# Reordering the head of a transformer layer: loads, statistics, weight splits and the first projection

## The chip, the cores and the metric

One core of a Trainium2 chip runs the whole kernel. The metric is the device time of one launch in microseconds, as the median of several runs. Lower is better.

## The reference

The input `x` holds 4 sequences (the code calls them blocks) of 256 tokens with 256 features. What is computed:

```
xn  = (x - mean) / sqrt(var + 1e-5)              # per token
q,k,v = xn @ Wqkv.T                              # 16 heads of 16 features
s   = softmax(q k^T / 4) v @ Wproj.T + bproj     # attention per sequence and head
h   = gelu(xn @ proj1.T + b1)                    # 1024 hidden features
g   = silu(h @ proj2.T + b2)
out = x + s * g
```

Everything is float32. The kernel gets that accuracy from TensorE in three products: each operand is split into a high part (rounded to the fast 32-bit matmul type) and a low part (the rest), and hi·hi, lo·hi and hi·lo are summed in PSUM.

## The kernel before, in words

Each engine has a program of its own, and a list that `build_order` writes out by hand gives all of them the same order of steps. Steps that matter here: `XT b` (transpose the normalised block `b` on TensorE), `QK h i` (project queries, i = 0 and 1, or keys, i = 2 and 3, of half `h`, which is 512 tokens or two blocks), `V`, `F1` and `F2` (values and the two layers of the feed-forward net), `S` (scores of two heads for the row maximum), `ST` (scores again, transposed, for the exponentials), `PV` and `PJ` (attention output and its projection).

The head of the kernel, which is what is changed, goes like this.

- SyncE (SP) issues the loads in the order x0, x1, the three thirds of `Wqkv` (queries, keys, values; 256 KB each, as an x block is), x2, x3, then `w1` (1 MB), and two small DMAs that write the rows of ones. ScalarE (ACT) issues three loads of the biases on its own queue at the very start; two of them are broadcast to 128 partitions.
- VectorE (DVE) does `norm_stats(b)` (two bn_stats, two bn_aggr, one add) and `norm_apply(b)` (two tensor_scalar, L484) for a block. Between them GpSimd (POOL) computes the reciprocal root in `rsqrt(b)` (L331).
- ACT makes the high part of a weight third in `split_wqkv(c)` (L379), POOL its low part (`wql`, L339).
- After `XT b` on TensorE (L632), ACT writes the high part `xTh` (L389) and DVE the low part `xTl` (L506).
- `QK 0 0` fills a PSUM bank of 512 columns in two products of 256 columns. ACT writes its high part to `stage` (L396), DVE its low part (L514), and only after both does SP issue three DMAs (L296) that restack the 128 rows of `stage` into groups of 16 partitions of `qs` or `ks`. There are 24 such DMAs of 256 KB, twelve for each half; `S` of a half waits for all its twelve (semaphore `stacked`, 192).
- SP works its list strictly in order: the twelve stack DMAs of half 0, the loads of `w2` and `wp`, then the twelve of half 1.

The order of DVE in the head before is: stats 0, stats 1, apply 0, apply 1, `xTl` of block 0, `xTl` of block 1, stats 2, stats 3, low part of `QK 0 0`, apply 2, low part of `QK 0 1`, apply 3. The order of POOL is: root 0, root 1, `wql` of the three thirds, root 2, root 3, `w1l`. The order of ACT is: high part of thirds 0 and 1, `xTh` of block 0, high part of third 2, `xTh` of block 1, then the high parts of `QK`.

Of the kernel before, what the change touches and what calls it, by code (L numbers as in the profile page):

```python
# [5 lines left out]
B, SQ, E = 4, 256, 256  # L6
NH, HN = 16, 16
F = 1024
P = 128
TOK = B * SQ  # L10
TT = TOK // P
HALF = TOK // 2
KC = E // P
# [79 lines left out]
def layer_kernel(nc, x, wqkv, w1, b1, w2, b2, wp, bp, out):  # L93
# [8 lines left out]
    with ctx:  # L102
# [168 lines left out]
        @block.sync  # L271
        def _(sp):

            x_t = x.rearrange("(b p t) e -> p b (t e)", p=P, t=2)
            out_t = out.rearrange("(b p t) e -> p b t e", p=P, t=2)
            for b in range(2):
                sp.dma_start(xs[:, 2 * b:2 * b + 2, :], x_t[:, b, :]).then_inc(x_in[b], 16)  # L277
            for c in range(3):
                sp.dma_start(wqkv_raw[:, c], wqkv[c]).then_inc(wqkv_in[c], 16)
            for b in range(2, B):  # L280
                sp.dma_start(xs[:, 2 * b:2 * b + 2, :], x_t[:, b, :]).then_inc(x_in[b], 16)
            sp.dma_start(w1_raw[:], w1).then_inc(w1_in, 16)
            sp.wait_ge(ones_ready, 1)
            for par in range(2):
                sp.dma_start(ks[64 * par + STK:64 * par + STM, :, :].bitcast(f32)
                             .rearrange("p h (b t) -> p (h b) t", t=SQ),
                             ones[0:2, None, :].to_broadcast([2, HP * B, SQ])).then_inc(ones_rows, 16)
            for h in range(2):
                cols = slice(h * HALF, (h + 1) * HALF)
                for i in range(4):  # L290
                    stack, parts = (qs, (0, 0, 1)) if i < 2 else (ks, (0, 1, 0))
                    sp.wait_ge(qk_hi, 4 * h + i + 1)
                    sp.wait_ge(qk_lo, 4 * h + i + 1)
                    for n, part in enumerate(parts):
                        row = 64 * (i % 2) + HN * n
                        sp.dma_start(stack[row:row + HN, :, cols].bitcast(f32),  # L296
                                     stage[:, h, i, part, :].bitcast(f32)).then_inc(stacked[h], 16)
                if h == 0:
                    sp.dma_start(w2_raw[:], w2).then_inc(w2_in, 16)
                    sp.dma_start(wps[:], wp).then_inc(wp_in, 16)  # L300
            for b in range(B):
                sp.wait_ge(m_hi, b + 1)
                sp.wait_ge(m_lo, b + 1)
                for qt in range(2):
                    for part in range(2):
                        c = b * SQ + qt * P
                        sp.dma_start(qs[STK + part:P:64, :, c:c + P].bitcast(f32),
                                     mm[qt * NH:(qt + 1) * NH, b % 2, part, :].bitcast(f32)).then_inc(m_rows[b], 16)
            sp.wait_ge(f1_made, 2 * FC)
            sp.dma_start(xb[:].rearrange("p (b t) e -> p b (t e)", t=2), x_t).then_inc(x_again, 16)  # L310
            for u in range(TT):
                sp.wait_ge(fin_done, u + 1)
                sp.dma_start(out_t[:, u // 2, u % 2, :],
                             fin[:, u % 4, :]).then_inc(stored[u], 16)
            for u in range(TT):
                sp.wait_ge(stored[u], 16)
# [3 lines left out]
        def _(pool):  # L320
# [8 lines left out]
            def rsqrt(b):  # L329
                pool.wait_ge(veps_done, b + 1)  # L330
                nc.gpsimd.tensor_tensor(rstd[:, 2 * b:2 * b + 2], veps[:, 2 * b:2 * b + 2],  # L331
                                        mhalf[:, 2 * b:2 * b + 2], ALU.pow).then_inc(rstd_done, 1)

            pool.wait_ge(mhalf_set, 1)
            rsqrt(0)
            rsqrt(1)
            for c in range(3):
                pool.wait_ge(wqkv_hi, c + 1)
                nc.gpsimd.tensor_tensor(wql[:, c], wqkv_raw[:, c], wqh[:, c].bitcast(f32),  # L339
                                        ALU.subtract).then_inc(wqkv_lo, 1)  # L340
            rsqrt(2)
            rsqrt(3)
            for kc in range(KC):
                pool.wait_ge(w1_hi, kc + 1)
                nc.gpsimd.tensor_tensor(w1l[:, kc, :], w1_raw[:, kc, :], w1h[:, kc, :].bitcast(f32),
# [22 lines left out]

        @block.scalar
        def _(act):  # L370
            act.dma_start(b1s[:], b1).then_inc(bias_in, 16)
            act.dma_start(b2s[:], b2.to_broadcast([P, E])).then_inc(bias_in, 16)
            act.dma_start(bps[:], bp.to_broadcast([P, E])).then_inc(bias_in, 16)
            act.wait_ge(warm_set, 1)
            nc.scalar.activation(rc[0:1, 0, 0, 0:1], warm[0:1, 0:1], ACT.Gelu)

# [2 lines left out]
                nc.scalar.activation(wqh[:, c], wqkv_raw[:, c], ACT.Copy).then_inc(wqkv_hi, 1)  # L379

            split_wqkv(0)
            split_wqkv(1)
            n_qk = n_v = n_f1 = n_mt = n_bt = 0
            for s in order:
                if s[0] == "XT":
                    b = s[1]
                    act.wait_ge(xt_made, b + 1)
                    for kc in range(KC):
                        nc.scalar.activation(xTh[:, kc, b * SQ:(b + 1) * SQ], xt_bank(b, kc),  # L389
                                             ACT.Copy).then_inc(xt_hi, 1)  # L390
                    if b == 0:
                        split_wqkv(2)
                elif s[0] == "QK":
                    h, i = s[1:]
                    act.wait_ge(qk_made, n_qk + 1)
# [71 lines left out]
        def _(dve):  # L467
# [25 lines left out]

            nc.vector.memset(warm[:], 0.0).then_inc(warm_set, 1)
            norm_stats(0)
            norm_stats(1)
            norm_apply(0)
            norm_apply(1)
            n_qk = n_mt = 0
            for s in order:  # L500
                if s[0] == "XT":
                    b = s[1]
                    cols = slice(b * SQ, (b + 1) * SQ)
                    for kc in range(KC):
                        dve.wait_ge(xt_hi, KC * b + kc + 1)
                        nc.vector.tensor_tensor(xTl[:, kc, cols], xt_bank(b, kc),  # L506
                                                xTh[:, kc, cols].bitcast(f32), ALU.subtract).then_inc(xt_lo, 1)
                    if b == 1:
                        norm_stats(2)
                        norm_stats(3)  # L510
# [77 lines left out]
        def _(pe):  # L588
# [18 lines left out]
            def wait_bank(s):  # L607
# [5 lines left out]
                else:  # L613
                    wait_free(pe, t_uses, t_free, s, 1)

            def warm_up():

                for _ in range(WARM):
                    nc.tensor.matmul(T[:, 0:HALF // 2], warm[:, 0:P], warm[:], start=True, stop=True)
# [4 lines left out]
            for s in order:  # L624
                if s[0] == "XT":
                    b = s[1]
                    if b >= 2:
                        pe.wait_ge(xt_lo, KC * (b - 1))
                    for t in range(2):
# [4 lines left out]
                    last.then_inc(xt_made, 1)  # L634
                elif s[0] == "QK":
                    h, i = s[1:]
                    pe.wait_ge(wqkv_hi, i // 2 + 1)
                    wait_free(pe, g_uses, g_free, s, 3)

                    cuts = [(0, SQ), (1, SQ)] if (h, i) == (0, 0) else [(h, HALF)]  # L640
                    for n, width in cuts:
                        cols = slice(n * width, (n + 1) * width)
                        seen = KC * (cols.stop // SQ - 1)
                        last = product(G[:, g_bank[s], n * width % HALF:n * width % HALF + width],
                                       lambda kc, a: (wqh, wql)[a][:, i // 2, kc, (i % 2) * P:(i % 2 + 1) * P],
                                       lambda kc, a: (xTh, xTl)[a][:, kc, cols], range(KC),
                                       rhs_hi=(xt_hi, seen), lhs_lo=(wqkv_lo, i // 2 + 1), rhs_lo=(xt_lo, seen))
                    last.then_inc(qk_made, 1)
                elif s[0] == "V":
                    h, p = s[1:]  # L650
                    pe.wait_ge(wqkv_lo, 3)
# [146 lines left out]
```

## Time and profile before

| | |
|---|---|
| runs of the kernel before | 163.93, 164.27, 165.26 us, median 164.27 |
| profiled execution, first to last instruction | 162.8 us |
| mean granted TensorE clock in it | 0.951 of full |
| TensorE busy / VectorE / ScalarE / GpSimd | 139.1 / 87.5 / 78.8 / 50.8 us |
| DMA | 13.28 MB in 7440 packets |

The span of the profiled execution is the time from its first to its last instruction. The time of a run holds something around it as well: 164.27 - 162.8 = 1.5 us, taken as fixed. Times in the sections below are counted from the start of the span.

### The profile page before, as it was taken

What the parts mean: (1) busy time and instruction counts of PE and PEld (TensorE: products, weight loads), DVE (VectorE), ACT (ScalarE), POOL (GpSimd) and SP (SyncE); (2) the same over time, 40 slices, a digit from 0 to 9 for tenths busy, and PEclk for the clock granted to TensorE, in tenths of its full rate; (3) what the DMA queues carried; (4) which work ended last, traced back from release to release, by engine and by line L of the source; (5) the groups of instructions that cost most, each with busy time, mean ns of one, the idle gap of its engine ahead of it and who ended that gap; (6) DMA issues with size and microseconds to landing.
All of it is one profiled execution on the core that took longest, in us unless ns stands there. A gap on an engine that the chain in (4) does not pass through costs nothing.

```text
span 162.8 us, 2711 instructions
## 1 busy us (share of the span) xinstructions
PE 139.1 (85%) x1028; PEld 100.7 (62%) x1028; DVE 87.5 (54%) x170; ACT 78.8 (48%) x115; POOL 50.8 (31%) x53
## 2 busy tenths in 40 slices
PE   7589799200199999999999999999999999999990
PEld 5378698100186666887876667865766666565570
DVE  2569935100046868787976867225245525645663
ACT  3074844100065566111136667787567756788600
POOL 3374920000039766300006666007942003300000
PEclk9999999975569999999999999999999999999997
DMA  5992999999999999960000000053000100001001
GB/s 130 259 380 48 140 119 121 119 120 122 238 202 122 123 124 123 123 78 1 10 2 2 0 8 4 2 154 114 0 0 8 60 0 4 9 26 38 32 30 67
DMA packets 7440, 13.28 MB, mean 82 GB/s; under 512 B 900, under 2 KB 2564, under 8 KB 7172
## 3 DMA queue, kind: packets, MB, share of 16 engines
q1 hardware_dynamic: 6996, 12.85, 45.8%
q10 hardware_dynamic: 432, 0.27, 1.4%
q8 instruction: 8, 0.13, 0.4%
q14 instruction: 4, 0.03, 0.1%
HBM read 5.51 MB, written 1.05 MB: 40 GB/s over the span
## 4 chain that ended last, share of the span: by engine, by line
PE 58%; DMA 21%; SPq 13%; DVE 3%; ACT 2%; issue 1%
PE G L603 31%; DMA ks<-stage 17%; SPq L296 12%; PE G L728 10%; PE SC L696 9%; DMA wqkv_raw<-wqkv 4%; PE SC L676 4%; PE T L737 2%; DVE xs L484 2%; PE G L744 1%; ACT stage L396 1%; DVE fin L582 1%; SPq L277 0%; ACT hG L428 0%; DVE stage L514 0%
## 5 line engine op out<-in xcount | busy, mean ns | idle before, releaser
L523 DVE TENSOR_REDUCE negm<-SC 128x4 f32<-128x1024 f32 x32 | 38.6, 1224 | 29.8 <-PE SC L676 29.4
L446 ACT ACTIVATE PT<-SC 128x1024 f32<-128x1024 f32 x32 | 32.7, 1023 | 11.1 <-PE SC L696 10.7
L354 POOL TENSOR_TENSOR hTl<-hG,hTh 128x512 fp32r<-128x512 f32 x16 | 20.5, 1284 | 29.0 <-ACT hTh L432 29.0
L676 PE MATMUL SC<-ks,qs 48*128 48x256 f32 x128 | 15.5, 331 | 14.9 <-DMA ks<-stage 14.9
L676 PEld LDWEIGHTS SC<-ks,qs 48*128 48x128 f32 x128 | 9.6, 191 | 22.5 <-DMA ks<-stage 15.3
L728 PE MATMUL G<-PT,VA 128*17 128x256 f32 x256 | 16.9, 382 | 0.3 <-DVE cd L535 0.3
L428 ACT ACTIVATE hG<-G,b1s 128x512 f32<-128x512 f32 x16 | 11.0, 688 | 12.1 <-PE G L603 12.1
L696 PE MATMUL SC<-qs,ks 50*128 50x256 f32 x128 | 16.1, 329 | 0.0
L603 PE MATMUL G<-w2h,hTh 128*128 128x256 f32 x64 | 15.2, 319 | 0.2 <-ACT hG L428 0.2
L696 PEld LDWEIGHTS SC<-qs,ks 50*128 50x128 f32 x128 | 9.5, 184 | 7.3 <-issue 5.0
L535 DVE COPY cd<-G 128x256 f32<-128x256 f32 x16 | 6.8, 425 | 12.4 <-PE G L728 12.1
L350 POOL TENSOR_TENSOR w2l<-w_raw,w2h 128x1024 fp32r<-128x1024 f32 x2 | 4.7, 2384 | 26.1 <-ACT w2h L415 26.1
L603 PE MATMUL G<-w2h,hTl 128*128 128x256 f32 x64 | 12.8, 282 | 0.0
L603 PE MATMUL G<-w2l,hTh 128*128 128x256 f32 x64 | 12.8, 282 | 0.0
L603 PEld LDWEIGHTS G<-w2h,hTh 128*128 128x128 f32 x64 | 9.7, 189 | 3.2 <-POOL hTl L354 0.4
L603 PE MATMUL G<-xTh,w1h 128*128 128x512 f32 x32 | 11.6, 445 | 0.0
L364 POOL TENSOR_TENSOR bg<-gate,bps 128x256 f32<-128x256 f32 x8 | 5.8, 729 | 17.5 <-DVE gate L491 16.6
L432 ACT ACTIVATE hTh<-hG 128x512 fp32r<-128x512 f32 x16 | 10.1, 632 | 0.5
L603 PE MATMUL G<-xTh,w1l 128*128 128x512 f32 x32 | 10.0, 394 | 0.0
L603 PE MATMUL G<-xTl,w1h 128*128 128x512 f32 x32 | 9.9, 392 | 0.0
L603 PEld LDWEIGHTS G<-w2l,hTh 128*128 128x128 f32 x64 | 9.9, 191 | 0.0
L415 ACT ACTIVATE w2h<-w_raw 128x1024 fp32r<-128x1024 f32 x2 | 2.0, 1048 | 16.3 <-DMA w_raw<-w 16.3
(83 smaller groups left out, 225.3 us busy)
## 6 DMA issues: line engine op xcount, KB each, us to landing
qs<-stage SPq DMA_DIRECT2D x12, 256.0 KB, 19.3
ks<-stage SPq DMA_DIRECT2D x12, 256.0 KB, 23.1
w_raw<-w SPq DMA_DIRECT2D x2, 1024.0 KB, 15.5
xs<-x SPq DMA_DIRECT2D x4, 256.0 KB, 6.1
xb<-x SPq DMA_DIRECT2D x1, 1024.0 KB, 5.5
out<-fin SPq DMA_DIRECT2D x8, 128.0 KB, 1.7
wqkv_raw<-wqkv SPq DMA_DIRECT2D x3, 256.0 KB, 7.0
wps<-wp SPq DMA_DIRECT2D x1, 256.0 KB, 24.5
```

Source lines behind the costliest of these rows:

```text
L296: sp.dma_start(stack[row:row + HN, :, cols].bitcast(f32), stage[:, h, i, part, :].bitcast(f32)).then_inc(stacked[h], 16)
L354: nc.gpsimd.tensor_tensor(hTl[:, n % FC, :], hG[:, n % FC, :], hTh[:, n % FC, :].bitcast(f32), ALU.subtract).then_inc(h_lo, 1)
L364: nc.gpsimd.tensor_tensor(bg[:, u % 2, :], gate[:, u, :], bps[:], ALU.mult).then_inc(bg_done, 1)
L428: nc.scalar.activation(hG[:, f, :], G[:, g_bank[s], :], ACT.Gelu, bias=b1s[:, f:f + 1]).then_inc(gelu_done, 1)
L432: nc.scalar.activation(hTh[:, f, :], hG[:, f, :], ACT.Copy).then_inc(h_hi, 1)
L446: nc.scalar.activation(PT[:, w % 4], SC[:, sc_slot[s]], ACT.Exp).then_inc(exp_done, 1)
L523: nc.vector.tensor_reduce(negm[:, b, :, :, hp].rearrange("p q a -> p a q"), SC[:, sc_slot[s]], axis=AX.X, op=ALU.max, negate=True).then_in ...
L535: nc.vector.tensor_copy(cd[:, g % 2, :], PV).then_inc(cd_out, 1)
L603: m = nc.tensor.matmul(dst, lhs(kc, a), rhs(kc, b), start=first and n == 0, stop=last and n == len(todo) - 1)
L676: last = nc.tensor.matmul(SC[:, sc_slot[s], par, qt, :], qs[rows, hp, c:c + P], ks[rows, hp, b * SQ:(b + 1) * SQ], start=True, stop=True)
L696: last = nc.tensor.matmul(SC[:, sc_slot[s], par, kt, :], ks[rows, hp, c:c + P], qs[rows, hp, b * SQ:(b + 1) * SQ], start=True, stop=True)
L728: last = nc.tensor.matmul(PV[32 * m:32 * m + VW, :], VA[:, 2 * b + kt, 4 * j + m, :], PT[:, w % 4, m % 2, kt, :], start=(kt == 0), stop=(k ...
```

## The change

Four things are done to the head; nothing after `QK 0 0` is touched.

1. SP issues x0, third 0, x1, third 1, x2, x3, third 2, `w1`, and then the three bias loads, which leave ACT's queue. The ones rows follow.
2. DVE does stats 0, apply 0, stats 1, `xTl` of block 0, apply 1, `xTl` of block 1, stats 2 and so on. POOL alternates: root 0, `wql` 0, root 1, `wql` 1, root 2, `wql` 2, root 3.
3. ACT splits third 0, writes `xTh` of block 0, splits third 1, writes `xTh` of block 1, splits third 2.
4. TensorE does the first 256 columns of `QK 0 0` between the transposes of block 0 and those of block 1.

```diff
-            for b in range(2):
-                sp.dma_start(xs[:, 2 * b:2 * b + 2, :], x_t[:, b, :]).then_inc(x_in[b], 16)
-            for c in range(3):
-                sp.dma_start(wqkv_raw[:, c], wqkv[c]).then_inc(wqkv_in[c], 16)
-            for b in range(2, B):
-                sp.dma_start(xs[:, 2 * b:2 * b + 2, :], x_t[:, b, :]).then_inc(x_in[b], 16)
+            load_x(0)
+            load_wqkv(0)
+            load_x(1)
+            load_wqkv(1)
+            load_x(2)
+            load_x(3)
+            load_wqkv(2)
             sp.dma_start(w1_raw[:], w1).then_inc(w1_in, 16)
+            sp.dma_start(b1s[:], b1).then_inc(bias_in, 16)
+            sp.dma_start(b2s[:], b2.to_broadcast([P, E])).then_inc(bias_in, 16)
+            sp.dma_start(bps[:], bp.to_broadcast([P, E])).then_inc(bias_in, 16)
...
             rsqrt(0)
-            rsqrt(1)
             for c in range(3):
                 pool.wait_ge(wqkv_hi, c + 1)
                 nc.gpsimd.tensor_tensor(wql[:, c], wqkv_raw[:, c], wqh[:, c].bitcast(f32),
                                         ALU.subtract).then_inc(wqkv_lo, 1)
-            rsqrt(2)
-            rsqrt(3)
+                rsqrt(c + 1)
...
-            act.dma_start(b1s[:], b1).then_inc(bias_in, 16)
-            act.dma_start(b2s[:], b2.to_broadcast([P, E])).then_inc(bias_in, 16)
-            act.dma_start(bps[:], bp.to_broadcast([P, E])).then_inc(bias_in, 16)
...
             split_wqkv(0)
-            split_wqkv(1)
...
-                    if b == 0:
-                        split_wqkv(2)
+                    if b <= 1:
+                        split_wqkv(b + 1)
...
             norm_stats(0)
+            norm_apply(0)
             norm_stats(1)
-            norm_apply(0)
-            norm_apply(1)
...
+                    if b == 0:
+                        norm_apply(1)
                     if b == 1:
                         norm_stats(2)
                         norm_stats(3)
...
+            def project(h, i, start, stop):
+                cols = slice(h * HALF + start, h * HALF + stop)
+                seen = KC * (cols.stop // SQ - 1)
+                pe.wait_ge(wqkv_hi, i // 2 + 1)
+                return product(G[:, g_bank[("QK", h, i)], start:stop],
+                               lambda kc, a: (wqh, wql)[a][:, i // 2, kc, (i % 2) * P:(i % 2 + 1) * P],
+                               lambda kc, a: (xTh, xTl)[a][:, kc, cols], range(KC),
+                               rhs_hi=(xt_hi, seen), lhs_lo=(wqkv_lo, i // 2 + 1), rhs_lo=(xt_lo, seen))
...
                 if s[0] == "XT":
                     b = s[1]
+                    if b == 1:
+                        project(0, 0, 0, SQ)
...
                     h, i = s[1:]
-                    pe.wait_ge(wqkv_hi, i // 2 + 1)
                     wait_free(pe, g_uses, g_free, s, 3)
-
-                    cuts = [(0, SQ), (1, SQ)] if (h, i) == (0, 0) else [(h, HALF)]
...
+                    first = SQ if (h, i) == (0, 0) else 0
+                    project(h, i, first, HALF).then_inc(qk_made, 1)
```

## Rows read from the trace of the kernel before

**Rows 1.** Chain that ended last, in order of time: start us, us, what.
```profile
15.58 0.69 DVE stage L514
...
46.13 27.37 DMA ks<-stage
```

**Rows 2.** TensorE timeline: start us, us, what, [idle before <-releaser].
```profile
44.10 0.80 PE L676 MATMUL SC<-ks,qs 48*128 48x256 f32 x4 [14.74 <-DMA ks<-stage]
...
73.54 0.50 PE L676 MATMUL SC<-ks,qs 48*128 48x256 f32 x4 [0.18 <-DMA ks<-stage]
```

**Rows 3.** Windows: busy us of each engine, PEclk, DMA share, GB/s.
```profile
44.10:73.40 29.30, 29.26 (x173) 22.05 (x173) 20.05 (x20) 13.62 (x21) 14.95 (x10) 0.93 1.02 134
...
11.50:16.00 4.50, 4.50 (x20) 3.92 (x20) 4.16 (x16) 1.65 (x3) 2.69 (x4) 1.00 0.21 58
16.00:44.00 28.00, 12.50 (x76) 10.78 (x74) 8.39 (x13) 7.80 (x15) 4.79 (x2) 0.83 1.08 132
```

**Rows 4.** Half-microsecond windows of the head, same columns.
```profile
4.50:5.00 0.50, 0.50 (x3) 0.41 (x2) 0.17 (x1) 0.00 (x0) 0.16 (x1) 1.00 0.76 82
...
9.00:9.50 0.50, 0.50 (x4) 0.25 (x2) 0.00 (x0) 0.34 (x1) 0.44 (x1) 1.00 1.14 463
...
15.50:16.00 0.50, 0.50 (x4) 0.42 (x3) 0.42 (x1) 0.50 (x2) 0.00 (x0) 1.00 0.08 14
```

**Rows 5.** DMA issues on SP's queue, timeline.
```profile
6.02 1.52 SPq L285 DMA_DIRECT2D ks<-ones  x2
14.76 3.87 SPq L296 DMA_DIRECT2D qs<-stage  x6
```

**Rows 6.** DMA view, 1.5 to 9 us: ACT's queue (q10), issue to landing.
```profile
q10 hardware_dynamic: 432, 0.27, 30.1%
```

**Rows 7.** VectorE timeline, 3.5 to 15 us.
```profile
3.51 0.75 DVE L472 BATCH_NORM_STATS2 stats<-xs 128x6 f32<-128x256 f32 x2 [2.38 <-DMA xs<-x]
...
6.00 0.75 DVE L472 BATCH_NORM_STATS2 stats<-xs 128x6 f32<-128x256 f32 x2 [1.31 <-DMA xs<-x]
7.08 0.73 DVE L484 TENSOR_SCALAR xs<-xs,mv,rstd 128x256 f32<-128x256 f32 x2
8.07 0.73 DVE L484 TENSOR_SCALAR xs<-xs,mv,rstd 128x256 f32<-128x256 f32 x2 [0.27 <-POOL rstd L331]
11.16 0.76 DVE L506 TENSOR_TENSOR xTl<-SC,xTh 128x256 fp32r<-128x256 f32 x2 [0.31 <-ACT xTh L389]
11.84 0.74 DVE L472 BATCH_NORM_STATS2 stats<-xs 128x6 f32<-128x256 f32 x2
13.98 0.68 DVE L514 SCALAR_TENSOR_TENSOR stage<-G,stage 128x512 fp32r<-128x512 f32 x1
```

**Rows 8.** GpSimd timeline, 4.8 to 19 us.
```profile
4.84 0.71 POOL L331 TENSOR_TENSOR rstd<-veps,mhalf 128x2 f32<-128x2 f32 x1 [2.83 <-DVE veps L477]
7.25 0.79 POOL L331 TENSOR_TENSOR rstd<-veps,mhalf 128x2 f32<-128x2 f32 x1 [1.70 <-DVE veps L477]
9.06 3.74 POOL L339 TENSOR_TENSOR wql<-wqkv_raw,wqh 128x512 fp32r<-128x512 f32 x3 [1.02 <-ACT wqh L379]
16.57 2.38 POOL L345 TENSOR_TENSOR w1l<-w_raw,w1h 128x1024 fp32r<-128x1024 f32 x1 [1.72 <-ACT w1h L402]
```

**Rows 9.** Tile xs: the normalising operation (min/median/max ns), and its slow pair on the timeline.
```profile
L484 DVE TENSOR_SCALAR xs<-xs,mv,rstd x8: 396/407/2595, 7.1 to 16.5; 128x256 f32<-128x256 f32 x8
...
16.18 2.92 DVE L484 TENSOR_SCALAR xs<-xs,mv,rstd 128x256 f32<-128x256 f32 x2
```

**Rows 10.** ScalarE timeline of the head.
```profile
8.36 0.63 ACT L379 ACTIVATE wqh<-wqkv_raw 128x512 fp32r<-128x512 f32 x1 [4.72 <-DMA wqkv_raw<-wqkv]
10.75 0.66 ACT L389 ACTIVATE xTh<-SC 128x256 fp32r<-128x256 f32 x2
13.14 0.60 ACT L396 ACTIVATE stage<-G 128x512 fp32r<-128x512 f32 x1 [1.74 <-PE G L603]
19.63 0.66 ACT L389 ACTIVATE xTh<-SC 128x256 fp32r<-128x256 f32 x2 [0.68 <-PE SC L632]
```

More of the change, by code:

```diff
@@ L275, in _, with load_x, load_wqkv @@
             out_t = out.rearrange("(b p t) e -> p b t e", p=P, t=2)
-            for b in range(2):
+            def load_x(b):
                 sp.dma_start(xs[:, 2 * b:2 * b + 2, :], x_t[:, b, :]).then_inc(x_in[b], 16)
-            for c in range(3):
+            def load_wqkv(c):
                 sp.dma_start(wqkv_raw[:, c], wqkv[c]).then_inc(wqkv_in[c], 16)
-            for b in range(2, B):
-                sp.dma_start(xs[:, 2 * b:2 * b + 2, :], x_t[:, b, :]).then_inc(x_in[b], 16)
+            load_x(0)
[5 more added lines that the diff above has]
+            load_wqkv(2)
             sp.dma_start(w1_raw[:], w1).then_inc(w1_in, 16)
+            sp.dma_start(b1s[:], b1).then_inc(bias_in, 16)
+            sp.dma_start(b2s[:], b2.to_broadcast([P, E])).then_inc(bias_in, 16)
+            sp.dma_start(bps[:], bp.to_broadcast([P, E])).then_inc(bias_in, 16)
             sp.wait_ge(ones_ready, 1)
@@ L636, in _ @@
                     h, i = s[1:]
-                    pe.wait_ge(wqkv_hi, i // 2 + 1)
                     wait_free(pe, g_uses, g_free, s, 3)
-                    cuts = [(0, SQ), (1, SQ)] if (h, i) == (0, 0) else [(h, HALF)]
[L641 to L648, printed above, removed]
+                    first = SQ if (h, i) == (0, 0) else 0
+                    project(h, i, first, HALF).then_inc(qk_made, 1)
                 elif s[0] == "V":
```

## The prediction

> **What bounds the kernel now.** I read the chain of waits first. Its long piece in the middle is a stack DMA (`ks<-stage`) that is issued at 46.13 us and lands at 73.5; the pieces just before the stack DMAs lead back through VectorE's low parts [rows 1]. The timeline of TensorE says the same more sharply: it is idle for 14.74 us until the first score at 44.10, because the twelve stack DMAs of half 0 have not landed, and it meets those of half 1 at 73.54 with 0.18 us to spare [rows 2]. Between these two points TensorE is busy 29.26 of 29.30 us [rows 3], and what comes later is a list of TensorE steps that the change doesn't touch. So the end stands at a fixed distance behind 44.10.
>
> What sets 44.10? From 16.0 to 44.0 the DMA engines are full (share 1.08, 132 GB/s); from 11.5 to 16.0 they are nearly empty (0.21) [rows 3], and in the half microsecond before 16.0 their share is 0.08 [rows 4]. The full stretch begins when SP issues the first stack DMA, at 14.76, with data moving 1.2 us later [rows 4, 5]. That DMA waits for the low part of `QK 0 0` on VectorE, which runs from 13.98 to 14.66 [rows 7]. Each later stack DMA finds a queue ahead of it: the three of `QK 0 0` alone are 768 KB, 6 us at 132 GB/s, and the second low part is there 1.6 us after the first [rows 1, 7]. The quantity to forecast is therefore one time: **when the low part of `QK 0 0` starts on VectorE** (13.98 now). A shift of it moves the full DMA stretch, 44.10 and the end by the same amount.
>
> Why is it at 13.98? The high part is written from 13.14 to 13.74 [rows 10], so VectorE comes 0.24 us late: it works through statistics 2 and 3 from 11.84 to 13.98, behind `xTl` of block 1 at 11.16, which follows `xTh` of block 1 at 10.75 [rows 7, 10]. VectorE and the arrival of block 1 are the bound, not TensorE.
>
> **The change, part by part.**
>
> *Loads.* Now the bias loads stand beside the first loads: ACT's queue takes 30.1% of the engines' time between 1.5 and 9 us, 2.3 us of all sixteen [rows 6], and the rate falls to 82 GB/s at 4.5 to 5.0 us where it is 463 GB/s at 9.0 to 9.5 [rows 4]. With the biases at the end of SP's list, x0 meets less traffic. It lands by 3.51 now, when its first statistics start [rows 7]; its issue and latency stay, so I take 0.15 us off, between 0 and 0.3. Third 0 comes right behind it: 256 KB at 463 GB/s is 0.6 us, so it lands near 4.1 instead of just ahead of its split at 8.36 [rows 10]. x1 and third 1 follow by some 5.3 instead of 6.00 and 9.16. The three bias issues add about 1.3 us to SP's list (0.76 each would be the price of the ones issues, 1.52 for two [rows 5]), and SP is idle from 7.54 to 14.76, which hides either. All other bytes are the same, and the biases are first waited for in `F1`, behind the first score.
>
> *Root 0 and apply 0.* Root 0 ends at 4.84 + 0.71 = 5.55 now [rows 8], so at 5.40. VectorE no longer does statistics 1 first; apply 0, now at 7.08, can start at 5.43. But POOL's next instruction is now `wql` 0 and not root 1. Its operand is the high part of third 0, ready at 4.1 + 0.63 = 4.7 [rows 10]. Both start at 5.4.
>
> *What happens when they overlap.* One place of the trace shows it. The normalising operation takes 407 ns in the median and 2595 ns at most, and the slow one lies in the pair at 16.18 (2.92 us instead of 0.73) [rows 9]. POOL's `w1l` starts at 16.57, just as the first of the pair ends, and lasts 2.38 us, to 18.95 [rows 8]; the pair ends at 19.10. VectorE's second operation stood still for the whole POOL instruction and ended 0.15 us behind it. Root 1 on POOL (0.79 us, beside apply 0 at 7.08) doesn't do that to VectorE [rows 7, 8], so it is the long subtraction over 128 partitions that does. In the kernel before, no `wql` meets an apply: the three run from 9.06 to 12.80, the applies end at 8.80 and resume later [rows 7, 8]. In the new order each apply is released by a root behind which a `wql` stands ready.
>
> The Trainium skill states this as a rule ("SBUF — State Buffer", section "Who interferes with whom"): a VectorE instruction in a two-port mode, which an fp32 tensor_scalar inside SBUF enters, and a GpSimd instruction exclude each other for a whole instruction, and the one that starts first wins. The trace agrees with it for the pair at 16.18 (2595 ns against 407); by the rule roots would block too, and the trace shows no such delay of VectorE.
>
> *The price.* One `wql` lasts 3.74 / 3 = 1.25 us [rows 8]. Whoever starts first, apply 0 ends near 5.40 + 1.25 + 0.15 + the second operation's 0.33, or 0.41 + 1.25 + 0.15: 7.2. (Now: 7.08 + 0.73 = 7.81. Without the meeting: 6.2.) From the start of statistics 1 to its root took 6.00 to 7.25 = 1.25 us, and the root 0.71 [rows 7, 8]; root 1 ends at 7.2 + 1.25 + 0.7 = 9.15. Meanwhile `xTh` of block 0 starts 0.53 us behind the apply (19.10 to 19.63 for block 3 [rows 9, 10]), at 7.75, and ends at 8.4; ACT splits third 1 until 9.05; VectorE does `xTl` of block 0 until 9.1. So `wql` 1 is ready just when root 1 ends, and apply 1 meets it too: it ends at 9.15 + 1.25 + 0.5 = 10.9, where it ends at 8.80 now. `xTh` of block 1 starts at 10.9 + 0.53 = 11.45 instead of 10.75 (now it waits there for ACT, which splits thirds 1 and 2 first). That is 0.7 us later, and everything that VectorE does from there to the low part of `QK 0 0` is unchanged: 13.98 + 0.7 = 14.7.
>
> *TensorE.* Half of `QK 0 0` is done while block 1 is still on VectorE. Now the high part starts (13.14) 1.73 us behind the end of `xTh` of block 1 (10.75 + 0.66) [rows 10], with nearly all twelve matmuls in between; from 12.1 that distance gives 13.85 and an end at 14.45, before 14.7, though only six are left. The early projection is hidden behind VectorE and saves nothing.
>
> *Root 2 behind `wql` 1, root 3 behind `wql` 2.* Root 2 waits for statistics 2 anyway. `wql` 2 now comes after it, near 14.3 to 15.6; `V` needs it behind `xTh` of block 3, at 19.63 now [rows 10]. Apply 2 may lose a few tenths, apply 3 may again stand behind `w1l`; both feed steps whose stack DMAs queue for over 6 us, and TensorE has 14.74 us to spare. Costed at nothing.
>
> *Sum.* +0.7 us on the first stack DMA, so a span of 163.5 and, with the 1.5 us around it, 164.27 + 0.7 = 165.0. Bounds: x0 landing 0.3 us earlier makes it +0.55; not at all earlier, +0.85.
>
> **The rivals.**
>
> *No meeting* (third 0 or its high part comes after apply 0 has started both operations, or the meeting costs little for a subtraction half as long). Then apply 0 ends at 6.2, root 1 at 8.1, apply 1 at 8.9, `xTh` of block 1 starts at 9.4 instead of 10.75, and the low part starts 1.3 us earlier. Not all of it may reach the end: two small DMAs of ones keep a share of 0.08 to 0.2 busy until 16.0 [rows 3, 4], that is, one to three engines which can't start on stack packets before. Between 0 and 1.3 us; with 1.2, 163.1. For it: the loads' arrival is an estimate. Against it: third 0 would have to land 0.7 us later than computed, and again for third 1.
>
> *One meeting.* If only one apply is held, the shift is 0.7 - 1.0 = -0.3: 164.0.
>
> *The ones rows behind the biases (slower).* On the engines that carry the ones rows, the stack packets queue behind biases and ones. Now the biases take 2.3 us of all engines while sharing them with other loads; alone at the end, at the 82 GB/s of their worst half microsecond [rows 4], their 0.27 MB take 3.3 us. The tail that now ends at 16.0 ends at 17.0. Stack data would start at 16.7 by my forecast, so from a bias time over 3.0 us this tail decides: with both, and with `wql` meeting twice, +1.0 to +1.8, 165.3 to 166.1. For it: the low rate while they run. Against: the first loads become faster by the same engine time, and the other engines can go ahead.
>
> *The DMA stretch doesn't follow its start* (its length is set by the slowest engines, those with the ones rows until 16.0): 164.3 as now for an earlier start; for a later one it follows.
>
> **How the numbers follow.** Two meetings 0.52 (165.0); one meeting 0.15 (164.0); none 0.18 (163.1); ones rows 0.10 (166.0); start without effect 0.05 (164.3). A measurement of this kernel can't tell less than about 1%, 1.6 us, from no change, and nearly all cases lie inside 162.6 to 165.9. Faster by over 1% needs no meeting and some other gain of the loads: 0.07. Slower by over 1% needs the ones rows at their worst or a third meeting on the path: 0.11. The range from 163.0 to 166.0 leaves out the low half of the first rival and the worst of the third.
>
> **What would show it.** In the profile of the changed kernel: a normalising operation of 1.3 to 1.7 us for block 0 and for block 1 beside a `wql` (against 407 ns); statistics 2 starting near 12.5; the first stack DMA issued at 15.4 to 15.5; the first score at 44.8; TensorE busy without a break behind it. If both applies take 0.73 us, or the first stack DMA goes out before 14.7, the forecast is wrong in sign; if it goes out at 15.5 and the first score still stands at 44.1, the link between the two is wrong. What could break it otherwise is a change in the speed of the full DMA stretch: 1% of its 57 us is 0.6 us.

## The result and the profile after

The changed kernel takes 166.65 us in the median of four runs (165.47 to 166.85), the kernel before 164.61 us (163.93 to 165.26) beside it: a ratio of 1.0108, with a 95% interval from 1.0061 to 1.0155. It is slower by 2.0 us in the medians (1.8 by the ratio), where 0.7 was forecast, and outside the range. Ratios are taken over the runs in the usual, faster state of the chip, so they are not exactly the quotient of the medians. The profiled execution has a span of 165.1 us, 2.3 more than before. Its own time is 166.85 us, so what lies around the span is 1.75 us and not the 1.5 taken above; the forecast rests on differences and does not change by that.

The quantity that the prediction made everything hang on is the first stack DMA. SP's queue of the changed kernel, timeline:

```profile
6.13 1.53 SPq L296 DMA_DIRECT2D ks<-ones  x2
16.77 3.87 SPq L307 DMA_DIRECT2D qs<-stage  x6
```

It goes out at 16.77 instead of 14.76 [rows 5]: +2.01. TensorE's timeline gives the first score:

```profile
46.16 0.80 PE L685 MATMUL SC<-ks,qs 48*128 48x256 f32 x4 [15.18 <-DMA ks<-stage]
```

46.16 against 44.10 [rows 2]: +2.06. The distance between the two is 29.39 us, and was 29.34. So between these two kernels the link that was forecast holds, and the lost time arose ahead of 16.77 us. VectorE's timeline of the head, changed kernel:

```profile
3.53 0.75 DVE L477 BATCH_NORM_STATS2 stats<-xs 128x6 f32<-128x256 f32 x2 [2.40 <-DMA xs<-x]
...
5.61 1.67 DVE L489 TENSOR_SCALAR xs<-xs,mv,rstd 128x256 f32<-128x256 f32 x2 [0.90 <-POOL rstd L342]
7.20 0.74 DVE L477 BATCH_NORM_STATS2 stats<-xs 128x6 f32<-128x256 f32 x2
...
9.16 1.75 DVE L489 TENSOR_SCALAR xs<-xs,mv,rstd 128x256 f32<-128x256 f32 x2
12.22 0.76 DVE L510 TENSOR_TENSOR xTl<-SC,xTh 128x256 fp32r<-128x256 f32 x2 [1.30 <-ACT xTh L394]
12.89 0.74 DVE L477 BATCH_NORM_STATS2 stats<-xs 128x6 f32<-128x256 f32 x2
13.55 0.30 DVE L480 BATCH_NORM_AGGREGATE mv<-stats 128x2 f32<-128x6 f32 x2
13.89 0.17 DVE L482 TENSOR_SCALAR veps<-mv 128x2 f32<-128x2 f32 x1
...
14.96 1.13 DVE L482 TENSOR_SCALAR veps<-mv 128x2 f32<-128x2 f32 x1
16.00 0.68 DVE L520 SCALAR_TENSOR_TENSOR stage<-G,stage 128x512 fp32r<-128x512 f32 x1
```

And GpSimd's:

```profile
4.86 0.71 POOL L342 TENSOR_TENSOR rstd<-veps,mhalf 128x2 f32<-128x2 f32 x1 [2.85 <-DVE veps L482]
5.54 1.27 POOL L349 TENSOR_TENSOR wql<-wqkv_raw,wqh 128x512 fp32r<-128x512 f32 x1
...
9.17 1.27 POOL L349 TENSOR_TENSOR wql<-wqkv_raw,wqh 128x512 fp32r<-128x512 f32 x1
14.13 0.69 POOL L342 TENSOR_TENSOR rstd<-veps,mhalf 128x2 f32<-128x2 f32 x1 [3.69 <-DVE veps L482]
14.79 1.28 POOL L349 TENSOR_TENSOR wql<-wqkv_raw,wqh 128x512 fp32r<-128x512 f32 x1
```

Lay the two beside each other. Three times a subtraction of 1.27 us stands on POOL, and three times a VectorE operation next to it is too long: apply 0 (1.67 instead of 0.73 us), apply 1 (1.75 instead of 0.73), and the little add of 1e-5 on 128x2 elements that ends statistics 3 (1.13 instead of 0.17, the row at 13.89 being its undisturbed twin). In the kernel before the applies took 0.73 us [rows 7], and the low part of `QK 0 0` could start at 13.98 and not at 16.00. Other operations of VectorE keep their length beside such a subtraction: in the kernel before, the three run from 9.06 to 12.80 [rows 8], and `xTl` (0.76 us twice) and bn_stats (0.74) are as long there as elsewhere [rows 7].

ScalarE's timeline shows a second thing, which I had taken too small:

```profile
4.22 0.63 ACT L385 ACTIVATE wqh<-wqkv_raw 128x512 fp32r<-128x512 f32 x1 [1.99 <-DMA wqkv_raw<-wqkv]
7.92 0.66 ACT L394 ACTIVATE xTh<-SC 128x256 fp32r<-128x256 f32 x2 [3.06 <-PE SC L650]
...
11.80 0.66 ACT L394 ACTIVATE xTh<-SC 128x256 fp32r<-128x256 f32 x2 [2.71 <-PE SC L650]
13.99 0.60 ACT L401 ACTIVATE stage<-G 128x512 fp32r<-128x512 f32 x1 [1.00 <-PE G L609]
```

`xTh` of block 1 starts 0.89 us behind the end of apply 1 (9.16 + 1.75 = 10.91), not 0.53. Between lie the transposes of block 1; TensorE's timeline of the changed kernel, and the window around it (busy us of PE, PEld, DVE, ACT, POOL, then granted clock, DMA share, GB/s):

```profile
10.65 1.12 PE L650 MATMUL SC<-ident,xs 128*128 128x128 f32 x4 [0.58 <-DVE xs L489]
```

```profile
7.50:17.50 10.00, 8.29 (x28) 6.49 (x27) 8.52 (x25) 3.90 (x9) 4.58 (x5) 0.50 0.39 143
...
15.00:18.00 3.00, 3.00 (x9) 2.35 (x8) 3.00 (x6) 1.45 (x2) 1.75 (x2) 0.54 0.00 0
```

The granted clock is 0.50 there, the lower of TensorE's two levels (1.2 of 2.4 GHz). TensorE had been idle from 5.03 us, the end of its warm-up matmuls, to 7.10. But the slowness itself is not new. The four transposes of block 1 took as long before, though the same window has a granted clock of 1.00 there:

```profile
8.54 1.11 PE L632 MATMUL SC<-ident,xs 128*128 128x128 f32 x4
12.48 0.63 PE L603 MATMUL G<-xTl,wqh 128*128 128x256 f32 x2
...
28.00 0.40 PE L603 MATMUL G<-wqh,xTl 128*128 128x256 f32 x2
```

These are rows of TensorE's timeline of the kernel before: a pair of 256-column matmuls takes 0.63 us at 12.48 and 0.40 at 28.00, so it too was slow in the head. It didn't matter there: the transposes were done at 9.65, and `xTh` of block 1 had to wait for ACT until 10.75.

The sum, on the first stack DMA: `xTh` of block 1 starts at 11.80 instead of 10.75 [rows 10], +1.05, and the stalled add is 0.96 longer. 1.05 + 0.96 = 2.01, all of the shift. (The last window of the changed kernel, 15 to 18 us, has a DMA share of 0.00: nothing else held the stack packets up.)

### The profile page after: what moved, and what is told of

The parts are those of the page before. It is cut to its first block, busy times and chain, and to the rows that moved or that the text cites. A ratio compares the mean times of both kernels' runs of the same rounds, so it can differ in the third digit from the quotient of the medians.

```text
span 165.1 us, 2712 instructions
## 1 busy us (share of the span) xinstructions
PE 140.7 (85%) x1028; PEld 101.7 (62%) x1028; DVE 90.1 (55%) x170; ACT 79.1 (48%) x115; POOL 50.7 (31%) x53
## 3 DMA queue, kind: packets, MB, share of 16 engines
HBM read 5.51 MB, written 1.05 MB: 40 GB/s over the span
## 4 chain that ended last, share of the span: by engine, by line
PE 69%; DMA 15%; DVE 10%; SPq 2%; issue 1%; POOL 1%; ACT 1%; POOLq 0%
PE G L609 39%; DMA ks<-stage 13%; PE G L737 10%; PE SC L705 8%; PE SC L685 8%; DVE xs L489 4%; PE T L746 2%; SPq L307 2%; DMA xs<-x 2%; DVE stats L477 2%; PE G L753 1%; DVE stage L520 1%; DVE veps L482 1%; POOL rstd L342 1%; PE SC L650 1%
## 5 line engine op out<-in xcount | busy, mean ns | idle before, releaser
L363 POOL TENSOR_TENSOR hTl<-hG,hTh 128x512 fp32r<-128x512 f32 x16 | 20.6, 1285 | 29.4 <-ACT hTh L437 29.4
L541 DVE COPY cd<-G 128x256 f32<-128x256 f32 x16 | 6.8, 425 | 12.5 <-PE G L737 12.3
L609 PE MATMUL G<-xTh,w1h 128*128 128x512 f32 x32 | 12.1, 462 | 0.0
```

The lines of the kernel that those rows point to most:

```text
L363: nc.gpsimd.tensor_tensor(hTl[:, n % FC, :], hG[:, n % FC, :], hTh[:, n % FC, :].bitcast(f32), ALU.subtract).then_inc(h_lo, 1)
L541: nc.vector.tensor_copy(cd[:, g % 2, :], PV).then_inc(cd_out, 1)
L609: m = nc.tensor.matmul(dst, lhs(kc, a), rhs(kc, b), start=first and n == 0, stop=last and n == len(todo) - 1)
```

## The experiments

Each group of kernels (e1 to e4, e5 to e8, e9 to e11) was timed beside the kernel before, on one chip for the group. "First stack" is SP's first issue of `qs<-stage`, "first score" TensorE's first matmul of `SC<-ks,qs`, both from the profiled execution.

| kernel | median us | ratio to before (95%) | span | first stack | first score | distance |
|---|---|---|---|---|---|---|
| before | | | 162.8 | 14.76 | 44.10 | 29.34 |
| changed | 166.65 | 1.0108 (1.0061 to 1.0155) | 165.1 | 16.77 | 46.16 | 29.39 |
| e1 root 3 first | 165.12 | 1.0027 (1.0005 to 1.0049) | 163.2 | 15.82 | 45.09 | 29.27 |
| e2 no meetings | 163.96 | 0.9961 (0.9940 to 0.9983) | 162.1 | 14.15 | 43.63 | 29.48 |
| e3 loads only | 164.72 | 1.0000 (0.9966 to 1.0034) | 163.1 | 15.86 | 44.83 | 28.97 |
| e4 orders only | 168.31 | 1.0221 (1.0186 to 1.0255) | 167.6 | 18.53 | 47.90 | 29.37 |
| e5 longer warm-up | 165.65 | 1.0041 (1.0005 to 1.0076) | 163.9 | 16.26 | 45.66 | 29.40 |
| e6 one meeting | 165.85 | 1.0078 (1.0039 to 1.0117) | 164.1 | 15.77 | 44.74 | 28.97 |
| e7 half splits | 164.88 | 0.9991 (0.9963 to 1.0020) | 162.8 | 15.60 | 44.54 | 28.94 |
| e8 low part first | 163.84 | 0.9919 (0.9887 to 0.9951) | 161.3 | 13.61 | 43.30 | 29.69 |
| e9 no early projection | 166.41 | 1.0115 (1.0075 to 1.0155) | 165.3 | 16.81 | 46.20 | 29.39 |
| e10 low part first, warm | 164.11 | 0.9974 (0.9946 to 1.0002) | 162.1 | 13.36 | 43.66 | 30.30 |
| e11 ones early | 171.55 | 1.0398 (1.0342 to 1.0454) | 168.7 | 12.79 | 48.89 | 36.10 |

The kernel before had a median of 164.55 beside e1 to e4, 164.98 beside e5 to e8, and 164.65 beside e9 to e11.

The last three columns come from one execution of each kernel, and the way from them to the time is looser than the prediction took it. The first stack DMAs of e1, e3, e6 and e7 lie within 0.26 us of each other (15.60 to 15.86), their ratios between 0.9991 and 1.0078. Two things vary besides the first stack DMA: the distance in the last column, and the time from the first score to the end of the span, which is 118.7 us in the kernel before and between 118.0 (e8) and 119.8 (e11) in the others. The second goes roughly with the granted clock in the 29.4 us behind the first score, where TensorE is busy without a break (28.25 of the 29.4 us in e11). The windows of e8, e6 and e4, whose ends lie 118.0, 119.4 and 119.7 us behind the first score:

```profile
43.30:72.70 29.40, 29.40 (x177) 22.21 (x177) 20.24 (x20) 13.64 (x21) 14.95 (x10) 0.94 0.99 130
```

```profile
44.74:74.14 29.40, 29.40 (x169) 22.11 (x170) 19.66 (x19) 13.63 (x21) 14.98 (x10) 0.90 0.99 136
```

```profile
47.90:77.30 29.40, 29.40 (x166) 22.01 (x167) 19.32 (x19) 13.63 (x21) 14.98 (x10) 0.89 0.94 132
```

Why the clock differs there was not tested. So the experiments show their causes on the first stack DMA; a difference of under about 1 us between two kernels' times can also come from behind the first score.

**e1: the third meeting taken away.** POOL's loop of the changed kernel:

```diff
             for c in range(3):
+                if c == 2:
+                    rsqrt(3)
                 pool.wait_ge(wqkv_hi, c + 1)
...
-                rsqrt(c + 1)
+                if c < 2:
+                    rsqrt(c + 1)
```

> The changed kernel, with POOL doing root 3 before the low part of third 2. Theory (meetings on VectorE and POOL cost the time, one subtraction each): the small add of statistics 3 takes 0.17 us again instead of 1.13, the low part of QK 0 0 starts near 15.0 instead of 16.00, the first stack DMA goes out near 15.8 instead of 16.77, and the first score and the end come 1.0 us earlier: about 165.6. Rival (the low granted clock of TensorE from 7.5 to 17.8 us sets the time, the stalled add only fills its shadow): the first score stays within 0.3 us of 46.2, time as the changed kernel.

VectorE's timeline of e1:

```profile
14.97 0.17 DVE L485 TENSOR_SCALAR veps<-mv 128x2 f32<-128x2 f32 x1
15.04 0.68 DVE L523 SCALAR_TENSOR_TENSOR stage<-G,stage 128x512 fp32r<-128x512 f32 x1
15.64 1.69 DVE L492 TENSOR_SCALAR xs<-xs,mv,rstd 128x256 f32<-128x256 f32 x2
```

The add is back at 0.17 us, the low part starts at 15.04, the first stack DMA 0.95 us earlier, the ratio falls from 1.0108 to 1.0027. TensorE is as slow as in the changed kernel (`xTh` of block 1 starts at 11.81, the high part at 13.99), so the rival (the stalled add fills the shadow of the clock) is out. The subtraction has only moved: now apply 2 is held by it (1.69 us), where nothing waits.

**e2: the three meetings taken away.** As e1, and in the same loop `pool.wait_ge(xn_done, 2 * c + 2)` ahead of the first two subtractions: they wait until VectorE has finished the apply.

> As e1, and POOL also waits for apply 0 before the low part of third 0, and for apply 1 before that of third 1. Theory: all applies take 0.73 us for a pair, apply 1 ends near 9.1 instead of 10.91, the low part of QK 0 0 starts near 13.2, the first stack DMA goes out near 14.0, 2.8 us before that of the changed kernel and 0.8 before that of the kernel before: about 163.8. Rival 1 (clock of TensorE): at most 1 us faster than the changed kernel. Rival 2 (the two DMA engines that carry the ones rows until about 15 us set the stretch): the first stack DMA goes out early, and the first score gains under 0.4 us on the kernel before.

```profile
5.61 0.73 DVE L494 TENSOR_SCALAR xs<-xs,mv,rstd 128x256 f32<-128x256 f32 x2 [0.90 <-POOL rstd L342]
...
7.25 0.46 DVE L487 TENSOR_SCALAR veps<-mv 128x2 f32<-128x2 f32 x1
...
8.52 0.73 DVE L494 TENSOR_SCALAR xs<-xs,mv,rstd 128x256 f32<-128x256 f32 x2 [0.15 <-POOL rstd L342]
...
13.37 0.68 DVE L525 SCALAR_TENSOR_TENSOR stage<-G,stage 128x512 fp32r<-128x512 f32 x1
```

In VectorE's timeline of e2 both applies take 0.73 us again. Two waits and a swap make a slower change a slightly faster one: 0.9961 of the kernel before, interval below 1. The first stack DMA goes out 0.61 us before that of the kernel before, and the first score gains 0.47 of it.

The kernel is not wholly free of meetings on the way to block 1. The wait has moved the subtraction of third 0 to 6.42 to 7.69 (POOL's timeline of e2), onto the add that ends statistics 1: it takes 0.46 us instead of 0.17, ends at 7.71, and root 1 starts only behind it, at 7.79. By estimate that costs apply 1 the 0.29 us by which the add is too long.

**e3: the loads alone.** The kernel before with the loads and bias loads of the changed one.

> The kernel before, with the loads and bias loads of the changed one and nothing else. Theory: the loads help by themselves. One meeting appears (root 1 releases apply 1 and the low part of third 0 at once), yet apply 1 ends near 8.7 as now, and ACT no longer waits for third 1, so xTh of block 1 starts near 9.4 instead of 10.75 and the first stack DMA goes out near 13.5: 163.2. Rival (biases at the end or the new order of the loads is what costs): slower than the kernel before, 165 or more.

A miss: no gain (1.0000), and the first stack DMA goes out at 15.86, 1.10 us later than in the kernel before. That the time is the same all the same comes from behind it: the first score is 0.73 later, and the span ends 118.3 us behind it instead of 118.7. VectorE's timeline of e3, with POOL's behind it:

```profile
6.37 0.75 DVE L480 BATCH_NORM_STATS2 stats<-xs 128x6 f32<-128x256 f32 x2 [1.70 <-DMA xs<-x]
...
7.46 0.73 DVE L492 TENSOR_SCALAR xs<-xs,mv,rstd 128x256 f32<-128x256 f32 x2
8.45 2.62 DVE L492 TENSOR_SCALAR xs<-xs,mv,rstd 128x256 f32<-128x256 f32 x2 [0.26 <-POOL rstd L342]
```

```profile
8.38 3.82 POOL L350 TENSOR_TENSOR wql<-wqkv_raw,wqh 128x512 fp32r<-128x512 f32 x3
```

Two things went otherwise than expected. x1 starts its statistics at 6.37 and not near 5 (6.00 before [rows 7]); third 0 now stands ahead of it in SP's list, which is the likely reason. And with the weights split early, POOL has its three subtractions in a row from 8.38, so apply 1 meets two of them, one for each of its operations: 2.62 us. Earlier loads by themselves bring a meeting that wasn't there before.

**e4: the orders alone.** The changed kernel with the loads of the kernel before.

> The changed kernel with the loads of the kernel before. Theory: third 0 lands at 8.3, so its low part doesn't meet apply 0, but root 1 now stands behind it in POOL's order until 11.0, apply 1 meets the low part of third 1 there, and statistics 3 meet that of third 2: the low part of QK 0 0 starts near 17.5, the end is 1 to 2 us behind the changed kernel: 167.5 to 168.5. Rival (the order of the loads costs the time, the orders of the engines are neutral): as the kernel before, 164.5.

```profile
9.05 1.27 POOL L338 TENSOR_TENSOR wql<-wqkv_raw,wqh 128x512 fp32r<-128x512 f32 x1 [3.46 <-ACT wqh L377]
10.29 0.69 POOL L331 TENSOR_TENSOR rstd<-veps,mhalf 128x2 f32<-128x2 f32 x1
```

The expectation holds (168.31): in POOL's timeline of e4 root 1 stands behind the subtraction until 10.98. The alternation on POOL needs the early loads; without them it is the worst of all the parts.

**e6: one meeting put into the kernel before.** On VectorE this is the cleanest test of the mechanism. Root 2 is moved ahead of the subtraction of third 2, and nothing else:

```diff
             for c in range(3):
                 pool.wait_ge(wqkv_hi, c + 1)
+                if c == 2:
+                    rsqrt(2)
                 nc.gpsimd.tensor_tensor(wql[:, c], wqkv_raw[:, c], wqh[:, c].bitcast(f32),
                                         ALU.subtract).then_inc(wqkv_lo, 1)
-            rsqrt(2)
             rsqrt(3)
```

> The kernel before with one swap in POOL's list: root 2 ahead of the low part of third 2, so that this subtraction may fall on the small add of statistics 3. Theory: third 2's low part starts at 13.8, the add at 13.9 ends with it near 15.1 instead of 14.07, the first stack DMA goes out near 15.8 and the end is 1.0 us later: 165.5. Rival (VectorE was stalled in the changed kernel by something else, such as the DMAs or the low clock): as before, 164.5.

VectorE's timeline of e6, then POOL's:

```profile
12.81 0.17 DVE L478 TENSOR_SCALAR veps<-mv 128x2 f32<-128x2 f32 x1
...
13.88 1.20 DVE L478 TENSOR_SCALAR veps<-mv 128x2 f32<-128x2 f32 x1
15.00 0.68 DVE L515 SCALAR_TENSOR_TENSOR stage<-G,stage 128x512 fp32r<-128x512 f32 x1
```

```profile
13.77 1.29 POOL L341 TENSOR_TENSOR wql<-wqkv_raw,wqh 128x512 fp32r<-128x512 f32 x1
```

The add starts 0.11 us behind the subtraction (13.77) and ends with it (15.08 against 15.06). The first stack DMA comes 1.01 us later, and the kernel is 0.78% slower (0.39 to 1.17). From 9 us to 13.8 VectorE and ScalarE start everything as in the kernel before, to 0.04 us. The end is less clean: of the 1.3 us that the span is longer, 0.64 lie in the first score and 0.66 behind it, with the granted clock of 0.90 there (0.93 in the kernel before, from 44.10 to 73.40 [rows 3]).

**e7: shorter instructions on POOL.** Each `wql` of the changed kernel in two subtractions of 256 columns.

> The changed kernel with every low part of a weight third done as two subtractions of 256 columns. Theory (an operation is held until the one POOL instruction ends, and may go in between two): a stalled small add waits at most 0.65 us instead of 1.13; an apply pair slips between the halves or waits for both, so it takes 1.4 to 2.0 us. Net 0.3 to 1.0 us below the changed kernel: 165.7 to 166.3. Rival (what holds VectorE is the total amount of POOL's traffic, not the instruction): the add waits 1.1 us again and the time stays.

```profile
14.16 0.73 POOL L349 TENSOR_TENSOR wql<-wqkv_raw,wqh 128x256 fp32r<-128x256 f32 x1
14.85 0.74 POOL L350 TENSOR_TENSOR wql<-wqkv_raw,wqh 128x256 fp32r<-128x256 f32 x1
```

```profile
14.33 0.58 DVE L483 TENSOR_SCALAR veps<-mv 128x2 f32<-128x2 f32 x1
```

POOL's timeline and VectorE's, both of e7: the add starts in the first half and ends at 14.91, just behind that half's end at 14.89, while the second half is at work. What holds VectorE is one POOL instruction, not the amount of work. The apply pairs take 1.54 us each, instead of 1.67 and 1.75. The first stack DMA comes 1.17 us earlier than in the changed kernel (0.55 of it from the add, 0.18 from x0 landing earlier in this execution, the rest from the pairs and the transposes), and the whole loss is gone: 0.9991. That is more than the 0.3 to 1.0 us expected. The span is 2.3 us shorter than that of the changed kernel: 1.17 of it in the first stack DMA, 0.45 in the distance, 0.68 behind the first score, and for the last two the experiment gives no cause.

**e5: the clock.** The changed kernel with `WARM = 9` instead of 5.

> The changed kernel with 9 warm-up matmuls instead of 5, so that TensorE works until about 6.8 us instead of 5.04. Theory: the granted clock stays at full for longer than 7.5 us; the transposes of block 1 then reach ACT 0.53 us behind the apply instead of 0.89, VectorE follows 0.3 to 0.4 us earlier, all three meetings stay: first stack DMA near 16.4, time 0.4 below the changed kernel, 166.2. Rival (the clock is the larger part of the loss): first stack DMA before 15.8 and over 1 us gained.

```profile
7.50:10.00 2.50, 1.32 (x8) 0.91 (x6) 2.31 (x8) 1.18 (x3) 1.63 (x2) 1.00 0.95 369
10.00:12.50 2.50, 1.44 (x7) 1.11 (x8) 1.55 (x5) 1.18 (x3) 0.29 (x1) 0.84 0.44 152
12.50:15.00 2.50, 2.50 (x10) 2.11 (x10) 2.43 (x10) 0.60 (x1) 1.37 (x2) 0.50 0.14 30
```

In the windows of e5 the granted clock stays at 1.00 until 10 us and falls only then. `xTh` of block 1 starts 0.53 us behind apply 1 (10.76 to 11.29), and the first stack DMA is 0.51 us earlier than in the changed kernel, with all three meetings in place. The transposes there take 0.76 us instead of 1.12. So TensorE's slower pace costs 0.36 us on this path (0.89 - 0.53), and 0.11 more at block 0; the kernel before has the same slow transposes, but only the changed one waits for them. The ratio falls further than expected, from 1.0108 to 1.0041 (about 1.1 us, 0.4 expected); 0.70 us of the 1.2 that the span is shorter lie behind the first score.

**e9: the early projection taken back.** The changed kernel with the first 256 columns of `QK 0 0` behind the transposes of block 1 again.

> The changed kernel with the first 256 columns of QK 0 0 back behind the transposes of block 1. Theory: the six matmuls take 1.3 us more behind xTh of block 1, so the high part ends near 15.9 instead of 14.6, just before VectorE comes to the low part at 16.0: the early projection gains nothing while the meetings are there, time within 0.3 us of the changed kernel, 166.6. Rival: TensorE's early work is what brings the clock down or delays the transposes of block 1, and without it the kernel is over 0.7 us faster; or the high part comes behind 16.0 and the kernel is slower.

First stack DMA 16.81 against 16.77, ratio 1.0115 against 1.0108: the early projection neither costs nor gains. Without it the high part ends at 14.98, still ahead of VectorE, which comes to the low part at 16.04.

**e8: a faster version.** e2, with statistics 3 moved on VectorE behind the low part of `QK 0 0`.

> The version without meetings, with statistics 3 behind the low part of QK 0 0 on VectorE. Theory: the high part ends at 12.93 there, so the low part starts near 12.95 instead of 13.37 and the first stack DMA goes out near 13.7: another 0.4 us, 163.5. Rival (the two DMA engines with the ones rows until 15 us, or a later step that needs block 3, take it back): no gain on the version without meetings.

```profile
12.83 0.69 DVE L524 SCALAR_TENSOR_TENSOR stage<-G,stage 128x512 fp32r<-128x512 f32 x1 [0.57 <-ACT stage L406]
```

In VectorE's timeline of e8 the low part now waits for ACT (0.57 us idle) instead of the other way round. 0.9919 of the kernel before, interval 0.9887 to 0.9951: the lowest ratio of the kernels tried, though its interval just meets that of e2 (0.9940 to 0.9983). The first stack DMA goes out 1.15 us before that of the kernel before, the first score gains 0.80.

**e10 and e11: two attempts to go on.** e10 is e8 with `WARM = 7`.

> The version without meetings and with the low part first, plus 7 warm-up matmuls instead of 5 (until about 5.9 us). Theory: transposes of block 1 reach ACT 0.3 us earlier at the full clock and the high part, which now sets the time, comes 0.3 to 0.8 us earlier: first stack DMA near 13.0, 163.4. Rival (the clock falls anyway or the ones rows on two DMA engines take the gain): as without, 163.8.

A miss. The warm-up now lies in front of the transposes of block 0, which were ready: it lasts until 7.48 instead of 5.81 in e8, and `xTh` of block 0 starts at 7.95 instead of 6.60. Its matmuls were also slow in this execution: 14 of them took 6.29 us on TensorE's timeline, where the 18 of e5 took 5.96. How much of the miss is due to that was not tested. The first stack DMA still goes out 0.25 us earlier than in e8, but the first score comes later; the distance is 30.30 us, the longest but for e11. In the windows of e10 the stack packets begin at 14.5 us, and before that there is a share of 0.14, about two engines of sixteen. I take it for the ones rows, the last DMAs ahead of the stack in SP's list; they were issued later than in e8 (6.69 instead of 6.38 us).

```profile
14.00:14.50 0.50, 0.50 (x4) 0.40 (x3) 0.47 (x4) 0.50 (x1) 0.07 (x1) 1.00 0.14 39
14.50:15.00 0.50, 0.50 (x4) 0.42 (x3) 0.50 (x3) 0.50 (x2) 0.50 (x1) 1.00 0.75 152
```

e11 puts the ones rows ahead of `w1`:

> The version without meetings and with the low part first, with the two DMAs of the ones rows ahead of w1 and the biases. Theory: the distance from the first stack DMA to the first score, 29.69 us there against 29.34 in the kernel before, comes back to 29.3, as no engine carries ones rows when the stack packets start: 0.3 us gained, 163.5. Rival 1 (those engines don't set the stretch): distance unchanged, time unchanged. Rival 2: w1 comes later on two engines by 4 us and ACT's split of w1 or POOL's low part holds block 3: slower.

Rival 2 decided, and far more than thought. The DMA view of e11 has `w1` landing 18.5 us after its issue at 5.58, where it took 7.6 in e8, and ScalarE's timeline shows who waits for it:

```profile
12.75 0.60 ACT L406 ACTIVATE stage<-G 128x512 fp32r<-128x512 f32 x1 [0.77 <-PE G L615]
24.08 1.06 ACT L412 ACTIVATE w1h<-w_raw 128x1024 fp32r<-128x1024 f32 x1 [10.74 <-DMA w_raw<-w]
25.05 0.58 ACT L406 ACTIVATE stage<-G 128x512 fp32r<-128x512 f32 x1
```

ACT's program splits `w1` between two high parts of `QK`, so the third high part waits 10.74 us for the load. The first stack DMA went out earlier than in any other kernel (12.79), but the third group, that of `QK 0 2`, only at 26.42 (21.39 in the changed kernel, whose first went out at 16.77). The DMA engines were not idle meanwhile: their share is over 1.0 from 14 to 26 us, and `w1`, which lands at 24.1, now lies inside the stretch beside the stack. Whether ones rows on two engines lengthen the stretch in e10 was not settled: among the others the distance varies by 0.75 us too.

## Why the prediction was wrong, point by point

- **The bound** (the start of the low part of `QK 0 0`, through the first stack DMA, to the first score and the end): right. Over eleven kernels with first stack DMAs from 13.61 to 18.53 (all but e10 and e11) the distance to the first score is 28.94 to 29.69 us. In the changed kernel 0.24 us of the 2.3 come behind the first score. What was too strong is "the end stands at a fixed distance behind 44.10": the time behind the first score was 118.0 to 119.7 us in these eleven, as wide as the change itself.
- **The loads:** third 0 is split at 4.22, forecast near 4.1. x0 landed no earlier than before (3.53), so the 0.15 us taken off weren't there (in other kernels with the same loads the first statistics started between 3.25 and 3.65). x1 and third 1 were forecast by some 5.3 and came later: in e3, where nothing hides them, statistics 1 start at 6.37 and the split of third 1 at 7.04, both released by their DMAs. In the changed kernel apply 0, held until 7.28, hides this.
- **The first two meetings:** right, and to 0.1 us. Apply 0 ends at 7.28, forecast 7.2; apply 1 ends at 10.91, forecast 10.9; root 1 at 9.12, forecast 9.15. e2 shows that they cost, since it takes them away: the first stack DMA goes out 1.67 us earlier than in e1, 0.09 of it from x0 landing earlier.
- **From apply 1 to `xTh` of block 1:** 0.53 us forecast, from block 3, at 19 us, when TensorE had its full pace; 0.89 measured. This is a mis-sized term, 0.36 us. The nearer row was there: the transposes of block 1 itself, 1.11 us in the kernel before.
- **The step that failed** is "Root 2 behind `wql` 1, root 3 behind `wql` 2 ... Costed at nothing." I looked for meetings only with the applies, whose slow example stood in the trace. But `wql` 2, put by the new order right behind root 2, starts while VectorE is in statistics 3, and these end in an add that is of the same kind as the apply, a tensor_scalar on fp32 in SBUF, if a tiny one. It cost 0.96 us on the first stack DMA. The Trainium skill's rule, which I had cited for the apply ("SBUF — State Buffer", section "Who interferes with whom"), names the operation, not its size, and would have led to the add; the trace agrees, with 1.13 us for an add that takes 0.17 alone. e1 takes it away and e6 makes it, alone, in the other kernel. Of the 2.01 us on the first stack DMA, 0.7 were forecast, 0.96 came from here and 0.35 from the transposes.
- **TensorE hidden:** right; the high part ends at 14.59 (forecast 14.45), and e9 shows the early projection to be worth nothing.
- **The rivals:** "no meeting" gave 163.1 in the forecast and 163.96 in e2, which stands for it, with a small meeting left; the low part started 0.61 us earlier than in the kernel before, not 1.3. Its reason against itself was right: third 0 was there in time. The ones rows behind the biases didn't decide here: from 15 to 18 us the DMA engines move nothing, and the stack DMA could have started. The DMA stretch followed its start: +2.06 on the first score for +2.01. "A third meeting on the path" was named as a mishap beside the slower case and given no price or place, though the trace had all it takes to place it.

## What to carry to other kernels

List every VectorE operation that a GpSimd instruction may hold up (here tensor_scalar operations on fp32 in SBUF were held, down to 128x2 elements), and go through the new order of both engines looking for each of them, not only for the long ones. Where a root released an apply on VectorE while a long subtraction stood ready behind it on POOL, the two met every time. A wait of the subtraction for the operation that it would hold removes the meeting, but look where the subtraction falls then: in e2 it fell on the next small add. Splitting it in two more than halved the delay of the add (0.41 us instead of 0.96), but took only 0.1 us off a pair of applies.

And when two edits go together (early loads, alternating orders), do each alone: here one was neutral in time, the other 2.2% slower, both together 1.1% slower, and with two waits and a swap more 0.4% faster.

## What the hardware showed that I had not expected

- An add on 128x2 elements that takes 0.17 us alone takes 1.13 and 1.20 us (changed kernel, e6) beside a GpSimd subtraction that started 0.17 and 0.11 us before it. A root on 128x2 elements on GpSimd does not hold VectorE noticeably: apply 0 of the kernel before takes 0.73 us beside root 1, which runs from 7.25 to 8.04 [rows 7, 8]. The root pays a little: in the traces of this case it takes 0.78 to 0.83 us when it starts beside an apply, and 0.69 to 0.71 when it doesn't.
- VectorE gets in between two GpSimd instructions that follow each other at once (e7, end at 14.91 inside the second half).
- The granted clock of the records and the pace of the matmuls can differ. The kernel before shows 1.00 from 7.5 to 17.5 us, e6 with the same head 0.50 from 10 to 12.5, and in both a pair of 256-column matmuls takes 0.63 us until 13 us. The durations are the surer sign.
- Drawing the warm-up out to the transposes (e5) kept TensorE's pace for the transposes of block 1 (0.76 us instead of 1.12). In e10 it was drawn out past the moment when those of block 0 were ready, and nothing was gained (0.9974 against 0.9919 in e8).
- A load of 1 MB issued behind two DMAs of 64 KB that go to two partitions each (e11) lands 18.5 us after its issue, against 7.6 us in e8, where it is issued ahead of them.
